# Second attention layer: the first head in two passes, and the row maxima of later steps one by one inside its blocks

## The reference

```python
q = (x @ Wq).reshape(B, S, HEADS, DIM_HEAD).transpose(0, 2, 1, 3)
k = (context @ Wk).reshape(B, L, HEADS, DIM_HEAD).transpose(0, 2, 1, 3)
v = (context @ Wv).reshape(B, L, HEADS, DIM_HEAD).transpose(0, 2, 1, 3)
attn = jnp.einsum('bhsd,bhld->bhsl', q, k) * scale
attn = jax.nn.softmax(attn, axis=-1)
out = jnp.einsum('bhsl,bhld->bhsd', attn, v)
out = out.transpose(0, 2, 1, 3).reshape(B, S, INNER)
return out @ Wo + bo
```

## Time and profile before

| | |
|---|---|
| Median of 3 runs | 1462.62 us (1462.29 to 1463.74) |
| The profiled execution | 1464.52 us |
| Its span in the profile | 1462.7 us |
| TensorE busy | 1391.6 us (95%) |
| VectorE busy | 1095.5 us (75%) |
| ScalarE busy | 793.9 us (54%) |
| GpSimd busy | 941.2 us (64%) |
| Lead-in, first to last reduction | 295.4 to 358.2 us |
| Head 0, from its first scores to head 1's first step | 361.3 to 488.6 us |

### The profile page before, as it was taken

How to read it: one execution, slowest core, us unless ns; L and a number is a source line. 1 busy time by engine, 2 the same in 40 slices (tenths; PEclk the granted TensorE clock), 3 DMA queues, 4 the chain that set the end, 5 groups by cost and what they waited for, 6 DMA issues and landing times.

```text
span 1462.7 us, 19933 instructions
## 1 busy us (share of the span) xinstructions
PE 1391.6 (95%) x6191; PEld 793.8 (54%) x6191; DVE 1095.5 (75%) x1484; ACT 793.9 (54%) x1576; POOL 941.2 (64%) x542
## 2 busy tenths in 40 slices
PE   5999998887999999999999999999999999998898
PEld 3877775533455555555554555455555555554565
DVE  8976666388888788778868878887887886666555
ACT  3458886321556556556655655555555555553332
POOL 5001113231889888978988897898898899886110
PEclk8999999655999999999999999999999999998799
DMA  6630000310000200100020020002002000000011
GB/s 173 206 126 18 18 17 7 71 22 2 0 1 1 49 1 1 33 17 1 1 49 1 1 46 4 1 1 49 1 0 47 1 1 1 1 1 13 18 38 40
DMA packets 77372, 39.45 MB, mean 27 GB/s; under 512 B 62047, under 2 KB 70000, under 8 KB 77002
## 3 DMA queue, kind: packets, MB, share of 16 engines
q1 hardware_dynamic: 77290, 38.36, 10.5%
HBM read 24.66 MB, written 13.68 MB: 26 GB/s over the span
## 4 chain that ended last, share of the span: by engine, by line
PE 86%; DVE 8%; DMA 3%; ACT 2%; issue 1%; POOL 0%; SPq 0%; ACTq 0%; DVEq 0%; POOLq 0%
PE ps L1384 24%; PE ps L1371 14%; PE ps L1372 12%; PE ps L1337 9%; DVE chunk_max L943 3%; DMA v_scratch<-v_stage 3%; PE ps L1324 3%; PE ps L1528 2%; PE ps L1199 2%; PE ps L1197 2%; PE ps L1208 2%; PE ps L1198 2%; PE ps L1209 2%; PE ps L1210 2%; PE ps L1316 1%
## 5 line engine op out<-in xcount | busy, mean ns | idle before, releaser
L524 POOL TENSOR_TENSOR psums<-psums,probs 126x1024 f32<-126x1024 f32 (+1 forms) x392 | 821.2, 2095 | 122.6 <-ACT probs L705 75.7
L705 ACT ACTIVATE probs<-ps 126x512 f32<-126x512 f32 (+1 forms) x816 | 416.2, 619 | 273.2 <-PE ps L1372 272.3
L943 DVE TENSOR_REDUCE chunk_max<-ps 128x2 f32<-128x1008 f32 (+1 forms) x416 | 472.7, 1181 | 77.1 <-PE ps L1337 75.7
L1384 PE MATMUL ps<-probs,v_mem 126*64 126x512 f32 (+1 forms) x1632 | 389.7, 598 | 0.0
L1371 PE MATMUL ps<-q_heads,ring 128*126 128x512 f32 (+1 forms) x816 | 342.9, 420 | 1.1
L1372 PE MATMUL ps<-q_low,ring 128*126 128x512 f32 (+1 forms) x816 | 322.5, 395 | 0.0
L994 DVE TENSOR_TENSOR xn<-xn,probs 126x512 f32<-126x512 f32 x126 | 231.1, 1834 | 29.9 <-ACT probs L705 25.6
L671 ACT CAST ring<-ps 64x252 fp32r<-64x252 f32 (+1 forms) x356 | 128.1, 360 | 136.3 <-PE ps L1324 133.2
L1384 PEld LDWEIGHTS ps<-probs,v_mem 126*64 126x64 f32 (+1 forms) x1632 | 111.5, 136 | 165.5 <-issue 120.9
L1371 PEld LDWEIGHTS ps<-q_heads,ring 128*126 128x126 f32 (+1 forms) x816 | 152.0, 186 | 88.6 <-issue 44.5
L1337 PE MATMUL ps<-ring,q_heads 64*128 64x504 f32 (+1 forms) x416 | 171.9, 482 | 18.1 <-DVE chunk_max L943 9.7
(11 more groups left out here) (200 smaller groups left out, 1412.8 us busy)
## 6 DMA issues: line engine op xcount, KB each, us to landing
v_scratch<-v_stage SPq DMA_DIRECT2D x51, 252.0 KB
v_mem<-v_scratch SPq DMA_DIRECT2D x8, 1606.5 KB
ctx_mem<-in_ctx_t SPq DMA_DIRECT2D x3, 803.2 KB, 8.9
vslot<-in_ctx_rows SPq DMA_DIRECT2D x51, 47.2 KB
pair_w<-in_f_pairs SPq DMA_DIRECT2D x17, 128.0 KB, 2.1
pair_w<-in_f_pairs SPq DMA_DIRECT2D x17, 65.0 KB, 1.8
x_tok<-in_x SPq DMA_DIRECT2D x1, 512.0 KB, 4.1
wo<-in_c_wo SPq DMA_DIRECT2D x1, 512.0 KB
```

Of the source, the lines that this page charges most:

```text
L524: pool.tensor_tensor(sums[0:r, 0:width], sums[0:r, 0:width], probs[0:r, n % PROBS, 0:width], ALU.add).then_inc(c_sum, 1)
L705: act.activation(probs[0:r, n % PROBS, cols(half)], ps[0:r, score_bank(t, half), :], ACT.Exp, scale=float(HD) ** -0.5).then_inc(c_exped, 1)
L943: dve.tensor_reduce(chunk_max[:, h % 2, i:i + 2, c], ps[:, banks[0]:banks[1] + 1, 0:group_tiles(c) * KT], AX, ALU.max).then_inc(c_reduced, 1)
L1384: ins = pe.matmul(ps[half * HD:(half + 1) * HD, B_ACC, :], v_tiles[0:r, h % 2, t, :], probs[0:r, n % PROBS, cols(half)], start=(t == 0), s ...
```

## The change

Head 0 is taken in two *passes*. Pass 0 is its first six blocks (24 tiles, `SPLIT = 6`), pass 1 the other seven; each has a maximum, a shift, an accumulation in bank 7 and a row of sums of its own. Pass p of later heads is p = h + 1. The two parts of head 0 are joined by *shares*: exp(scale (m_p − max(m_0, m_1))), times one reciprocal of the joined sum; `add_output` multiplies each pass's output with its share. The lead-in so holds only the 24 steps of the first six groups, and its nine `k_proj` stand behind every second step instead of every fourth. The other 28 steps of head 0 and all 52 of head 1 stand in head 0's first 12 blocks, 7 to a block (6 in blocks 4, 6, 7 and 8): one before the scores, on pair (5, 6); three (or two) in the middle, one behind the scores of each of the first three (two) tiles, all on pair (5, 6); two behind, one on each pair; and one *late*, among the values, ahead of the last tile's, on pair (3, 4). Block 12 and the later heads keep two before and two behind. In head 0 GpSimd adds all sums at full width and VectorE none (`by_vector`). The queries of head 2 move from blocks 5 and 6 to 6 and 7 in head 0. In head 1 the output of pass 1 is added in blocks 8 and 9, beside that of pass 0 in blocks 2 and 3.

```diff
+SPLIT = 6
+SPLIT_T = SPLIT * GT
+def pass_of(h, t):
+    return h + 1 if h or t >= SPLIT_T else 0
...
 def steps_in(h, b):
+    if h == 0 and b < GROUPS_H - 1:
+        small = [c for c in range(b) if first_head_small(c)]
+        at = SPLIT * STEPS + 7 * b - len(small)
+        middle = 2 if first_head_small(b) else 3
+        steps = list(range(at, at + 4 + middle))
+        return steps[:1], steps[1:1 + middle], steps[1 + middle:3 + middle], steps[3 + middle:]
...
-    middle = [GROUPS_H * STEPS + b] if h == 0 and b < STEPS else []
-    return steps[:2], middle, steps[2:]
+    return steps[:2], [], steps[2:], []
+def first_head_small(b):
+    return b in (4, 6, 7, 8)
+def queries_in(h):
+    return 5 if h else 6
+def output_in(p):
+    return 8 if p == 1 else 2
 def by_vector(h, t):
-    return h == HEADS - 1 or t % GT == GT - 1
+    return h == HEADS - 1 or h and t % GT == GT - 1
...
@@ scalar @@
+            def acc_out(p):
+                act.wait_ge(c_attended, tiles_until(p))
+                if p >= 2:
+                    act.wait_ge(c_out, 2 * (p - 1))
+                act.copy(acc_raw[:, p % 2, :], ps[:, B_ACC, :]).then_inc(c_acc, 1)
...
+                    if b == SPLIT and h == 0:
+                        acc_out(0)
...
+                    if h == 0 and b in (0, 1):
+                        q_rows(b + 1)
+                    if h == 0 and b == 5:
+                        act.wait_ge(c_mix, 2)
+                        act.activation(first_share[:, :, :], first_share[:, :, :], ACT.Exp,
+                                       scale=float(HD) ** -0.5).then_inc(c_mix, 1)
...
@@ vector @@
-            for step in range(GROUPS_H * STEPS):
-                maxima(step, step, FIRST_PAIRS[step % 3])
+            for step in range(SPLIT * STEPS):
+                maxima(step, FIRST_PAIRS[step % 3])
...
                     for k, step in enumerate(behind):
-                        maxima(step, count + k, PAIRS[k])
+                        maxima(step, PAIRS[k])
                     g = projected_in(h, b)
                     if g is not None:
                         k_lo(g, B_KEYS)
+                    for step in late:
+                        maxima(step, PAIRS[0])
...
@@ tensor @@
-                if step % STEPS == 1 and early < AHEAD:
+                if step % 2 and early < AHEAD:
                     k_proj(early)
...
+            def free_pair(k):
+                pe.wait_ge(c_reduced, last_on[k])
+                if k and pending:
+                    pe.wait_ge(*pending)
...
                     for k, step in enumerate(before):
+                        pair = 1 if len(before) == 1 else k
+                        free_pair(pair)
...
+                        max_scores(step, PAIRS[pair])
+                        last_on[pair] = step + 1
                     for t in block_tiles(b):
                         for half in range(2):
-                            scores1(h, t, half, reduced - len(before) // 2)
-                        if t % GT == 2:
...
+                            scores1(h, t, half, last_on[0])
+                        if t % GT < len(middle):
+                            step = middle[t % GT]
+                            free_pair(1)
+                            pending = None
+                            max_scores(step, PAIRS[1])
+                            last_on[1] = step + 1
+                        elif t % GT == 2:
+                            free_pair(1)
...
+                        if t % GT == 2:
+                            for step in late:
+                                free_pair(0)
+                                max_scores(step, PAIRS[0])
+                                last_on[0] = step + 1
```

More of the change, by code:

```diff
@@ L509, in _ @@
             for h in range(HEADS):
-                sums = psums[:, h % 2, :]
-                for t in range(1, TILES):
+                for t in range(TILES):
+                    p = pass_of(h, t)
+                    first = first_tile(p)
+                    if t == first:
+                        continue
+                    sums = psums[:, h % 2, :] if p else psums_0
                     n, r = TILES * h + t, rows_of(t)
@@ L1001, in add_rows @@
                     dve.tensor_tensor(sums, probs[0:KT, (n - 1) % PROBS, HALF:TOK], new, ALU.add).then_inc(c_sumd, 1)
-            count = GROUPS_H * STEPS
             for h in range(HEADS):
                 for b in range(GROUPS_H):
-                    before, middle, behind = steps_in(h, b)
+                    before, middle, behind, late = steps_in(h, b)
                     for k, step in enumerate(before):
-                        maxima(step, count + k, PAIRS[k])
+                        maxima(step, PAIRS[1 if len(before) == 1 else k])
                     if h == HEADS - 1:
@@ L1278, in _ @@
                 k_proj(g)
-            pe.wait_ge(f_mask, 1)
+            pe.wait_ge(f_step, 5)
             for t in range(TT):
@@ L1384, in attend1, with sum_rows @@
                     ins = pe.matmul(ps[half * HD:(half + 1) * HD, B_ACC, :], v_tiles[0:r, h % 2, t, :],
-                                    probs[0:r, n % PROBS, cols(half)], start=(t == 0), stop=(t == TILES - 1),
+                                    probs[0:r, n % PROBS, cols(half)], start=first, stop=last,
                                     skip_group_check=True)
                 ins.then_inc(c_attended, 1)
-            def sum_rows(h):
-                pe.wait_ge(c_sum, adds_to(h, TILES - 1 if h == HEADS - 1 else TILES))
+            def sum_rows(p):
+                h = head_of(p)
+                pe.wait_ge(c_sum, adds_to(h, SPLIT_T - 1 if p == 0 else TILES if 1 < p < HEADS else TILES - 1))
                 pe.wait_ge(c_sumd, vector_done(h, TILES - 1))
                 for t in range(TT):
-                    rows = psums[:, h % 2, tile_cols(t)]
+                    rows = psums[:, h % 2, tile_cols(t)] if p else psums_0[:, tile_cols(t)]
                     if h == HEADS - 1 and t >= TT // 2:
@@ L1397, in sum_rows, with project_out @@
                 ins.then_inc(c_sums, 1)
-            def project_out(h, part, banks):
+            def project_out(p, part, banks):
+                h = head_of(p)
                 if part == 0:
-                    pe.wait_ge(c_acc, h + 1)
-                    pe.wait_ge(c_rden, h + 1)
+                    pe.wait_ge(c_acc, p + 1)
+                    pe.wait_ge(c_rden, max(p, 1) + 1)
                 for u in (2 * part, 2 * part + 1):
@@ L1434, in _ @@
             pe.wait_ge(c_kfull, AHEAD)
-            count = GROUPS_H * STEPS
+            last_on = [SPLIT * STEPS, SPLIT * STEPS]
+            pending = (c_shift, 2)
+            def free_pair(k):
+                pe.wait_ge(c_reduced, last_on[k])
+                if k and pending:
+                    pe.wait_ge(*pending)
             for h in range(HEADS):
                 for b in range(GROUPS_H):
-                    before, middle, behind = steps_in(h, b)
+                    before, middle, behind, late = steps_in(h, b)
@@ L1442, in _ @@
                     for k, step in enumerate(before):
[L1443 to L1448 removed]
+                        pair = 1 if len(before) == 1 else k
+                        free_pair(pair)
+                        if pair:
+                            pending = None
```

275 lines of the change are left out of this document (158 added, 117 removed).

## The result

The changed kernel takes 1486.15 us (median of 4 runs, 1483.24 to 1488.60) against 1463.18 us before (1462.29 to 1464.93): ratio 1.0155, 95% interval 1.0129 to 1.0180. It is slower, as forecast, but by 23 us where the forecast said 6, and outside the stated range. The profiled execution has a span of 1486.5 us against 1462.7, 23.8 more, and the time splits at marks that both traces have: the end of the lead-in's last reduction, then the start of `acc_out` at the end of each head. One run of experiment e3 was disturbed (2671 us against 1470 to 1477 for the other three) and is left out of its figures.

What follows compares the result with a forecast made beforehand. It took the lead-in as bound by the maxima on VectorE and the heads by TensorE's order of work. Lead-in −29, head 0 +33 and head 1 +2.3 gave +6.3 us, say 1468.5 us; range for 8 in 10 1459 to 1476.

Steps and rivals of the forecast that it cites:

- The sign: Whole kernel: the change makes it slower, chance 0.56, against 0.24 faster and 0.20 same.
- the main mechanism: Head 0: steps on one pair come every 1.83 us against 1.56 of TensorE work, blocks 12.3 us, head 33 us more.
- the output of the second pass: Head 1, blocks 8 and 9: two added project_out and the waits behind them cost 1.0 us each.
- The first rival: Head 0: waits for the pair vanish, blocks take 11.5 us, head 0 loses 23 us, total 1459.2; chance 0.26.
- The third rival: Head 0: VectorE falls behind, each block's first reduction 0.5 us late, 6 us more, 1474.5; 0.66 together with the forecast.
- five small VectorE instructions in a row ... 0 to 0.5: Head 1: reciprocals becomes five instructions, the step behind waits for the last, costing 0 to 0.5 us.
- the new rounds hold TensorE busy all the time while it is slow, so it should rise early: Lead-in: the clock rises early, so the saving is taken as 29 us, nearer to the high clock.
- The working for low clock: Lead-in: two steps with their projection take 3.14 us, 39 us in all, ending at 333.7, saving 24.5 us.
- the ends of 24 and 32: Lead-in: bounds in us on the saving, from low clock (24.5) and high clock (31.7), around the 29 taken.
- The second rival: Head 0: the clock falls inside blocks, some 2 us a block, 24 in all, total 1492; chance 0.08.
- The rule of the Trainium skill cited for it: Head 0: short idles between groups of matmuls make the clock swing, so blocks waiting on one pair would lose clock.

Runs made afterwards that it cites:

- e3: Changed kernel with all 52 steps of head 0 back in the lead-in, keeping two passes: 1474.75 us (median of 3).
- e2: Changed kernel with reductions of head 0's before and middle steps reading half the columns, matmuls kept: 1476.19 us (one run).
- e4: Changed kernel with the joined sum in PSUM and head 0's same steps spaced over both pairs of banks: 1465.94 us (median of 10).
- e1: Changed kernel with the joined sum of head 0's two passes kept in PSUM instead of SBUF: 1477.07 us (median of 4).
- e6: Changed kernel with the lead-in's nine key projections computing only half their columns: 1480.01 us (one run).
- e7: Spaced kernel, joined sum in PSUM, eight blocks in pass 0, with head 1's queries moved from the lead-in to head 0's blocks 0 and 1: 1460.36 us.

## Why the prediction missed

**What held.** The sign, and the main mechanism: one pair of banks takes a step each 1.83 us (forecast 1.83, from 0.57, 1.22 and 0.04 of the earlier trace rows), TensorE has 1.56 us of work in that time (e2 shows it bare; the 0.21 in the rows counts from the modelled end of the matmul before), a block takes 12.34 us (forecast 12.3), and head 0 comes to +35.3 (forecast +33). Of the miss there, 1.6 us are block 8: 15.27 us against 13.7, because the clock fell. In head 1 the output of the second pass cost 0.8 and 1.3 us in blocks 8 and 9 (forecast 1.0 each). The first rival, waits that vanish, was wrong for this order of steps; its price of a block, 11.5 us, came only with the steps spaced over both pairs (e4). The third rival, VectorE falling behind, did not come: the reductions of the middle steps start 0.57 us after their steps.

**First failure: head 1, 8.8 for 2.3 us, the largest.** The failed step is the price of `reciprocals`, "five small VectorE instructions in a row ... 0 to 0.5": it has no row behind it, and never asked what the instructions read. There are four, not five; at about 0.2 us each (the reciprocal's 0.21 before) they would come to 0.84, which is what e1 measured. The chain was 4.65 us, plus TensorE's clock after a stop of 3.3 us. The warning stood in the trace before. These are rows of its timeline of VectorE, then of GpSimd's, an addition on each, both from SBUF:

```profile
484.85 0.67 DVE L994 TENSOR_TENSOR xn<-xn,probs 126x512 f32<-126x512 f32 x1
514.42 2.67 DVE L994 TENSOR_TENSOR xn<-xn,probs 126x512 f32<-126x512 f32 x1
```

```profile
482.48 2.37 POOL L524 TENSOR_TENSOR psums<-psums,probs 126x1024 f32<-126x1024 f32 x1
485.29 4.97 POOL L524 TENSOR_TENSOR psums<-psums,probs 126x1024 f32<-126x1024 f32 x2 [0.45 <-POOL psums L524]
...
511.65 9.09 POOL L524 TENSOR_TENSOR psums<-psums,probs 126x1024 f32<-126x1024 f32 x4 [2.27 <-ACT probs L705]
```

The same shape takes 0.67 us where it starts as a GpSimd addition ends (482.48 + 2.37 = 484.85), and 2.67 us in the middle of a run of four, begun 0.24 us after the second of them (514.18 to 516.54). e1 takes the cause away, and head 1 then costs the forecast 2.3.

**Second failure: the lead-in, −23.3 for −29.** The failed step is "the new rounds hold TensorE busy all the time while it is slow, so it should rise early". They did hold it busy, 9.7 to 9.9 of 10 us from 300 to 320, and the clock stayed at 0.50 until past 330, where the lead-in was all but over. The working for low clock was good (a round 3.14 us forecast, 3.32 measured, because from a step to the next projection it is 0.76 us and not the 0.58 that the sum took; saving 24.5 forecast, 23.3 measured); the choice between the ends was not, and cost 4.5 of the 5.7 us. The saving lies just outside the ends of 24 and 32 that the prediction gave it. e6 shows that the projections bind there.

**Third: the end of the span, +2.6 for 0.** The last layer has the same instructions in both. From the last mark on, its work ran at 0.67, 0.67 and 0.66 in the changed kernel's windows from 1380 to 1410 us, and at 0.72, 0.79 and 0.87 in the windows before from 1360 to 1390, which lie about as far behind that mark; after them both stand at 1.00. The last window of each, before and then changed:

```profile
1380.00:1390.00 10.00, 10.00 (x33) 6.47 (x32) 4.33 (x6) 3.33 (x6) 1.37 (x2) 0.87 0.08 20
```

```profile
1400.00:1410.00 10.00, 10.00 (x25) 6.04 (x24) 2.68 (x4) 1.67 (x3) 0.64 (x1) 0.66 0.00 0
```

I count it to the clock, which differs from run to run, not to the change: e6 has the changed kernel's code from head 0 on, and took 122.3 us here, as before (clock 0.70, 0.81 and 0.85), while e1 and e2 took 124.9. Why it differs is not shown.

**The second rival** had its place, though not its price. In plain blocks, which wait 0.21 us ahead of three steps, the windows show 1.00 throughout; the clock fell only where three such waits met `sum_rows`, and after the 3.3 us stop. The rule of the Trainium skill cited for it, small idles between groups of matmuls that make the clock swing, agrees with block 8, where short waits go ahead of one fall (0.88; with the waits taken away 1.00 in e2), and not with the other blocks. In block 8 it cost at most the 1.6 us of the miss, where this rival had 24 for head 0.

Misses by size: 6.5 in head 1, 5.7 in the lead-in, 2.6 at the end, 2.3 in head 0, 0.4 between, in all 17.5 of 23.8 us; the forecast had the other 6.3.

**What stays open.** What makes the clock rise in one lead-in and not in another, with the same instructions and the same busy TensorE (e4 against the changed kernel), was not found. Busy time alone is not it: in e7 TensorE was busy for 10.00 and 9.97 of 10 us from 300 to 320, and the clock stayed at 0.50.

## What to carry to other kernels

A step that must wait for its own buffer has a period, here matmul to reduction to release; if the work between two such steps is shorter, moving the steps apart is worth as much as halving their reductions: the same seven steps cost 12.34 us a block with five in a row on one pair, 11.48 with half reductions (e2), and 11.45 in full but spread over two pairs (e4). Before pricing a small VectorE instruction by its size, look at its operands and at what GpSimd is doing: with two SBUF operands it may last as long as the GpSimd instruction beside it, and the engine that waits for a chain of such instructions pays for each; with one operand in PSUM the wait was gone (e1). And when work is packed into a stage that runs at TensorE's low clock, price it at that clock: here that sum came within 1.2 us, and the hope that a busy TensorE would bring the clock up was what failed.

## What the runs showed of the hardware

A VectorE addition of 128x8 numbers from SBUF took 1.95 us beside a GpSimd addition and 0.17 us with one operand in PSUM; the same shapes from SBUF took 0.17 us each at 400.75 and 400.95 in the changed kernel, where GpSimd's last addition had ended at 400.14. TensorE's clock stayed at 0.50 from 300 to past 330 us while the engine was busy 9.86 and 9.73 of 10 us in the first two windows. VectorE's copy of 126x512 numbers, with one input, from SBUF, took 0.41 us in the changed kernel, and 1.67 (e1) and 2.16 us (before) where it began during a GpSimd addition; it then ended 0.29 and 0.28 us after that.
